# First block of a gated block kernel: idle transposes at the start, key spreads split over two queues, clears moved behind exponentials

## The reference: what is computed

```python
x = x + tanh(g_xattn) * attention(layernorm(x), ctx_1024, ctx_1024)
x = x + tanh(g_ffn)   * expert_layer(layernorm(x))
# attention: 16 heads of 16 features; queries from layernorm(x), keys and values from ctx
scores = q @ k.T                       # blocks of 128 queries
valid  = causal within the block       # (with the block before, where there is one)
o      = softmax(scores) @ v ; out = o @ wo.T + bo
# expert layer: softmax over 8 experts, the best 2 of them, at most 640 tokens an expert
y = (silu(xn @ Wg.T) * (xn @ Wu.T)) @ W3.T   # D=256, FF=1024
```

## Time and profile before

| | us |
|---|---|
| median of 3 runs | 522.09 |
| lowest and highest | 521.87, 523.62 |
| the profiled execution | 520.82 |
| its span, first to last instruction | 519.1 |
| outside the span (520.82 - 519.1) | 1.7 |

### The profile page before, as it was taken

One profiled execution on the slowest core, in us unless ns is written; L12 is line 12 of the kernel. 1 busy time (PEld: TensorE's weight loads), 2 busy tenths in 40 slices (PEclk: granted clock), 3 DMA queues, 4 the chain that ended last, 5 costly groups with the idle time before them and its releaser, 6 DMA issues.

```text
span 519.1 us, 10685 instructions
## 1 busy us (share of the span) xinstructions
PE 480.4 (93%) x3584; PEld 444.2 (86%) x3584; DVE 352.2 (68%) x864; ACT 295.7 (57%) x747; POOL 189.6 (37%) x257
## 2 busy tenths in 40 slices
PE   5989999999999997399999999999999999999991
PEld 3777888888878776399999999999999999999991
DVE  5597779888897998658775754676744858534340
ACT  5877877687778773437574633555643737324140
POOL 7518455776868477600403031112122030320302
PEclk9999999999999996589999999999999999999996
DMA  5989321414143611272857470465622473200111
GB/s 164 249 189 296 73 42 53 77 61 101 47 79 69 199 62 44 71 265 82 248 161 195 135 193 2 97 222 98 220 38 36 128 188 129 32 11 11 19 12 20
DMA packets 41650, 57.34 MB, mean 110 GB/s; under 512 B 3721, under 2 KB 38576, under 8 KB 39552
## 3 DMA queue, kind: packets, MB, share of 16 engines
q1 hardware_dynamic: 35008, 48.49, 32.0%
q0 software_dynamic: 6144, 8.07, 9.2%
q10 hardware_dynamic: 448, 0.14, 0.2%
HBM read 36.24 MB, written 16.72 MB: 102 GB/s over the span
## 4 chain that ended last, share of the span: by engine, by line
PE 55%; DVE 3%; issue 1%; POOL 1%; DMA 0%; DVEq 0%; ACT 0%; POOLq 0%
PE bank L1489 18%; PE bank L1490 17%; PE bank L1491 17%; PE bank L1483 2%; PE bank L1413 1%; DMA expert_rows<-xr,slotu 0%; POOL out_tokens L549 0%; DVE ysc L1181 0%; DVE xr L841 0%; DVE xr L839 0%; DVE topi L882 0%; DVE pT L945 0%; DVE bXl L1138 0%; DVE top L854 0%; DVE xr L900 0%
## 5 line engine op out<-in xcount | busy, mean ns | idle before, releaser
L549 POOL DMA_INDIRECT out_tokens<-ysc,rows x32 | 50.1, 1567 | 242.3 <-DVE ysc L1181 235.8
L1490 PE MATMUL bank<-bXl,wh 128*128 128x384 f32 (+1 forms) x384 | 121.8, 317 | 0.6 <-issue 0.6
L1489 PE MATMUL bank<-bXh,wh 128*128 128x384 f32 (+1 forms) x384 | 121.9, 318 | 0.3 <-DVE bXl L1138 0.3
L1491 PE MATMUL bank<-bXh,wl 128*128 128x384 f32 (+1 forms) x384 | 121.8, 317 | 0.0
L762 ACT ACTIVATE sil<-bank 128x384 f32<-128x384 f32 (+1 forms) x96 | 43.8, 456 | 125.9 <-PE bank L1491 125.8
L1160 DVE TENSOR_TENSOR hF<-sil,bank 128x384 f32<-128x384 f32 (+1 forms) x96 | 48.9, 510 | 75.5 <-ACT sil L762 75.2
L633 ACT ACTIVATE p<-bank,nm 128x128 f32<-128x128 f32 x256 | 73.6, 383 | 26.3 <-DVE nm L940 26.2
L1489 PE MATMUL bank<-wh,hH 128*128 128x256 f32 x256 | 73.8, 288 | 0.3 <-DVE ysc L1181 0.3
L1491 PEld LDWEIGHTS bank<-bXh,wl 128*128 128x128 f32 x384 | 72.6, 189 | 0.7 <-issue 0.7
L1489 PEld LDWEIGHTS bank<-bXh,wh 128*128 128x128 f32 x384 | 72.7, 189 | 0.5 <-issue 0.5
L1490 PEld LDWEIGHTS bank<-bXl,wh 128*128 128x128 f32 x384 | 72.7, 189 | 0.0
(11 more groups left out here) (144 smaller groups left out, 829.6 us busy)
## 6 DMA issues: line engine op xcount, KB each, us to landing
stage<-in_w12T SPq DMA_DIRECT2D x16, 1024.0 KB, 4.9
stage<-in_w3T SPq DMA_DIRECT2D x8, 1024.0 KB, 5.6
expert_rows<-padrow SPq DMA_DIRECT2D x8, 662.5 KB, 8.6
rows<-expert_rows SPq DMA_DIRECT2D x7, 662.5 KB, 4.3
kM<-k SPq DMA_DIRECT2D x62, 64.0 KB, 2.4
cT<-in_ctxT SPq DMA_DIRECT2D x8, 256.0 KB, 3.3
out_tokens<-x_all SPq DMA_DIRECT2D x8, 256.0 KB, 2.3
x_all<-in_x SPq DMA_DIRECT2D x2, 640.0 KB, 5.3
```

The costliest lines, as they stand in the source:

```text
L549: pool.indirect_dma_start(out=out, out_offset=bass.IndirectOffsetOnAxis(rows[par][:, c, D + E:ROW].bitcast(U32), 0), in_=ysc[par][:, c, :] ...
L1489: nc.tensor.matmul(out_ap, ah, bh, start=start, stop=False)
L1490: nc.tensor.matmul(out_ap, ah, bl, start=False, stop=False)
L1491: return nc.tensor.matmul(out_ap, al, bh, start=False, stop=stop)
```

## The change

Four things in the first block, none in the later ones:

1. TensorE gets idle transposes (`keep_running`) into bank Tb[0]: 6 behind the wait for the identity and ahead of the first keys, 1 between keys and input columns, and 4 between input columns and queries.
2. Spreads 6 and 7 of block 0 are issued by ScalarE and no longer by SyncE; each of the two issues 4.
3. ScalarE's clear of quarter 1 of kM[1]'s low part moves behind the queries.
4. Quarters 2 and 3 are cleared behind the exponentials of groups 0 and 1 in `body(0)`.

```diff
@@ SyncE
             sp.wait_ge(km_zero[0], 3)
-            spread_keys(0, 0, (0, 1, 4, 5, 6, 7))
+            spread_keys(0, 0, (0, 1, 4, 5))
             load_w(wo, woT, ld_wo)
@@ ScalarE, body
                     if cur:
                         exps(G, g, not prev1 and g < 2)
+                    if g < 2 and cur and not prev1:
+                        zero_low_keys(2 + g)
                     if g == 0 and cur:
                         values2(n, par)
@@ ScalarE, ahead of body(0)
             act.wait_ge(dve_kl, 1)
             act.wait_ge(km_zero[0], 3)
-            for a in (2, 3):
+            for a in (2, 3, 6, 7):
                 r = slice(a * HD, (a + 1) * HD)
-                act.dma_start(kM[0][r, :, a:H:HR, :].bitcast(F32), k2[r, :, :, :].bitcast(F32)).then_inc(ld_km[0], 16)
-            zero_low_keys(1)
+                act.dma_start(kM[0][r, :, a:H:HR, :].bitcast(F32), k2[r, :, :, :].bitcast(F32)).then_inc(ld_km[a // GH], 16)
             act.wait_ge(bias_ok, 1)
             queries(0, 0, Q0)
-            zero_low_keys(2)
+            zero_low_keys(1)
             values(0, Xo)
             values1(0, 0)
-            zero_low_keys(3)
             body(0, 0, False, False, True, True)
@@ TensorE
             pe.wait_ge(ident_ok, 1)
+            keep_running(Tb[0], 6)
             pe.wait_ge(ld_wk, 16)
             keys(0, 0, K0, 1)
+            keep_running(Tb[0], 1)
             input_columns(0, True, False)
+            keep_running(Tb[0], 4)
             pe.wait_ge(ld_wq, 16)
             queries(0, Q0)
```

## The result

| | before | after |
|---|---|---|
| median of the runs, us | 522.04 (4 runs) | 525.35 (4 runs) |
| lowest and highest | 521.87, 523.62 | 525.06, 525.82 |
| the profiled execution | 520.82 | 525.06 |
| its span | 519.1 | 523.4 |

The ratio of after to before is 1.0057, 95% interval 1.0036 to 1.0078. The change makes the kernel 2 to 3 us slower. Forecast was 521.8 with a range of 520.7 to 523.2; the measured median lies above it.

A forecast was written before the change was run, and what follows sets the result against it. TensorE was taken as bound once dense, some 25 to 27 us in. A 1.0 us lead at exponentials 0, mostly paid back by two clears, left 0.25 us: 522.09 - 0.25 = 521.8 us, range 520.7 to 523.2.

The forecast's parts named there:

- the dense point: Where TensorE's list becomes dense, some 25 to 27 us in; only moving it was to count, 0.25 us earlier.
- The idle transposes' own cost: First block, TensorE: waits for weights, x and queries hide the eleven transposes, cost taken as 0.
- the gain by the clock: Block 0's queries on TensorE: clock rises before them, so 1.97 us instead of 3.75; upper bound 1.8 us taken.
- The rest of the chain: First block, ScalarE and TensorE: spreads issued by 14.17, exponentials 0 at 18.06, pT at 24.6, block 1's queries at 27.0.
- Landing of the spreads: Block 0's spreads 0 to 3 land by 15.9 us, before scores at 16.1; up to 0.4 us allowed.
- payback step: ScalarE behind exponentials 0: two clears of 0.97 us each use up 1.13 us of slack; pT only 0.25 us earlier.
- The issue of spreads one after another: Rival, first block: shared generator issues eight spreads in turn, pT 2.4 us later, 524.5 us; chance 0.04.
- SyncE's pace: First block: SyncE's six spreads issue at 0.74 us each throughout, so both engines issue at the same time.
- The clock late: Rival, first block: clock does not rise before the queries while clears remain, 0.6 us later, 522.7 us; chance 0.22.
- The lead carried: Rival: the 1.0 us lead at exponentials 0 goes through to the end, 521.1 us; chance 0.15.
- Something not seen: Rival: an effect outside the listed cases, no size given; chance 0.04.
- The forecast's list of what would prove it wrong: Block 1's queries moved over 0.8 us, or such a difference only at the attention-expert pause, 195 to 225 us.

The follow-up runs named there:

- after_again: The changed kernel, unaltered, compared a second time with the kernel before: 523.32 against 521.13 us, ratio 1.0036.
- only_placed: Kernel before with 22 wait-only instructions ahead of TensorE's first work: 523.55 against 521.15 us, ratio 1.0046.
- no_idle: Changed kernel without its eleven idle transposes, compared with the kernel before: 521.33 against 521.15 us, ratio 1.0014.
- only_idle: Kernel before with the eleven idle transposes and nothing else of the change: 521.53 against 521.15 us, ratio 1.0005.
- idle_clears: Kernel before plus idle transposes and moved clears, spreads unmoved, wide idle products at 219 us bringing expert code back: 521.14 against 521.97 us, ratio 0.9977.
- after_code_back: Changed kernel with most old idle transposes at 219 us replaced by three wide products, against the kernel before: 520.35 against 521.13 us, ratio 0.9980.
- idle_spreads: Kernel before plus the eleven idle transposes and spreads 6 and 7 on ScalarE, clears unmoved: 524.54 against 521.13 us, ratio 1.0068.
- placed_10_late: Kernel before with 10 wait-only instructions in TensorE's idle wait at 215 to 219 us: 522.62 against 521.97 us, ratio 1.0003.
- code_back_only: Kernel before with most idle transposes at 219 us replaced by three wide products, expert code 40 instructions earlier: 525.29 against 521.97 us, ratio 1.0044.
- placed_22_late: Kernel before with 22 wait-only instructions in TensorE's idle wait at 215 to 219 us: 523.55 against 521.97 us, ratio 1.0017.
- placed_90_further: Changed kernel with 45 more tiny products (90 instructions) ahead of body(0), compared with the kernel before: 525.37 against 521.15 us, ratio 1.0083.

## Why the prediction was wrong

**The step that failed first** is the sentence that the change is worth what it moves the dense point "and nothing else in the 520 us". The idle transposes' own cost was put at 0, with the wait for the weights as their cover. As work that is right: the keys start at 5.54. As code they push every later jump 22 instructions on. Taken between the starts of the two matmuls at the border, less the 0.17 us of one, the hole costs 2.43 and 2.66 us in after and after_again, and 0.75, 0.32 and 0.41 in the three profiles of before: means of 2.55 and 0.49. Missing term: +2.1 us.

**The step that failed second** is the gain by the clock. I read from one execution that the first block runs at the low clock up to 14.8 us, and took that for the kernel. In eight profiles of kernels whose first block has the order of before and no transposes, the queries of block 0 took 1.97 us (once 1.96) in six and 3.5 to 3.75 us in two. Queries of block 1 started at 25.9 to 26.2 in five of the six (26.74 in only_placed, which has its extra waits) and at 27.25 and 27.75 in the two. The mean of the eight is 26.5. With transposes the queries were at 1.97 in all eight profiles, so they may well make the clock sure, but eight of eight against six of nine does not prove it. And the 1.8 us that I counted for it are there only in the executions in which the clock would have come late, here 2 of 8 (3 of 9 with no_idle).

**The rest of the chain held.** Four spreads on ScalarE end at 14.17 (forecast), queries at 14.28 (measured). Scores 16.1, and 16.30. Exponentials 18.06, and 18.24. pT of group 1 24.6, and 24.82. Queries of block 1 27.0, and 27.20, 27.21, 27.32, 27.00 in the four kernels that have the whole first block of the change. Only the mark that they are measured against was wrong: not 27.25, but 26.5 on average. So the dense point moves by +0.7 us and not by -0.25. Even against its own mark of 27.25 the gain was 0.05 us in the profile of after. Landing of the spreads was put at 15.9 with up to 0.4 allowed on top, and all of that was needed: the scores wait for the last one to 16.3. From issue to landing (min/median/max) SyncE's spreads took 3.6/3.9/4.0 us in after, against the 2.4/2.7/3.7 of the earlier trace rows. Taken one by one, the two that SyncE issued beside ScalarE's in the kernel before took 3.6 and 3.7 us, the third 3.0, and the last three, issued alone, 2.4 to 2.5. With four on each queue all of them have company. This cost only 0.1 us, since the queries' low part allows the scores at 16.2 in any case.

**Part by part**, from only_idle's 26.03: the clears' move gives 26.67 (idle_clears), the split added to it 27.20. Both parts cost. The clears cost 0.76 us because two of them (1.94 us) go into 1.1 us of slack, as the prediction's payback step worked out. The split costs 0.5 us because ScalarE comes to its queries later (14.28 against 12.93): their low part ends at 16.10 in after, where idle_clears has it at 14.76 and waits for the spreads up to 15.77. In after_again and after_code_back, too, it is this low part that the scores wait for (16.31 and 16.10), and the late landing adds 0.1 us in after. Beside unmoved clears it costs 2.2 us (idle_spreads), of which 0.3 are a late start and 0.8 the fallen clock.

**The sum as it should have been:** +0.7 and +2.1 make +2.8 us, where 3.3 and 2.2 were measured in the two comparisons. The sum is an estimate: its marks are means over single profiled executions.

**The rivals.** The issue of spreads one after another falls: four spreads took 2.88 us on ScalarE, 0.72 each, while SyncE issued its own at 0.77 each, against 0.70 and 0.74 in the earlier trace rows; the exclusive generator of which the Trainium skill tells in Perfetto Trace Analysis (DMA Instruction, HWDGE) does not show at this pace. One reading of the prediction was too coarse, though: SyncE's pace was not the same over all six. The first three took 0.75 to 0.85 us each and the last three 0.60 to 0.63. Whether ScalarE's issues beside them made the first ones slower, these runs do not tell: in after the fourth took 0.60 us while ScalarE was still issuing. The clock late did not come true in any profile of the change. The lead carried did not either. "Something not seen", given 0.04, was the case. The forecast's list of what would prove it wrong named 195 to 225 us as the place; the hole is 30 us behind that. And the row that was to show the forecast wrong, the queries of block 1, stood at 27.20 in after, 0.2 us from its forecast: it was no guard against a loss that comes later.

**What belongs to one execution.** In the first profile of after, TensorE waits at 216.76 where before had 214.72:

```profile
216.76 0.59 PE L1471 MATMUL bank<-member,onesb 128*128 128x8 bf16 x16 [2.29 <-DVE slotu L935]
```

In after_again, the same kernel:

```profile
214.62 0.59 PE L1471 MATMUL bank<-member,onesb 128*128 128x8 bf16 x16 [0.88 <-DVE slotu L935]
```

Behind the long one VectorE starts 1.4 us late on a finished product. It stands in four of 17 profiles (after, placed_10_late, code_back_only, idle_clears), half of it in a fifth (placed_22_late), and the other twelve have 0.88 or 0.89. The kernels with and without it don't fall apart by the change. What makes it stays open. So does what sets the clock's rise at 223 to 227 us, which moves the first expert matmuls by up to 0.6 us.

**What the terms leave.** Worked out in the same way, from the row of block 1's queries, the hole and the fallen clock where there is one, the medians of all compared kernels but the first after lie lower than the terms give, by 0.2 us (idle_spreads) to 1.0 (only_placed) and 1.2 (only_idle). One cause may be the mark: the three profiled executions of before took 520.82, 519.65 and 521.20 us, on average 0.8 us under the medians that belong to them (522.04, and 520.97 twice), so that the rows describe a kernel before that is faster than its median. The waits of 1.4 us above may be another, as they also fall on kernels whose code up to there is that of before (placed_10_late, code_back_only). Neither was measured.

## What to carry to other kernels

Instructions that cost no engine time still move all code behind them, and here the 22 of the idle transposes cost 2.1 us in the expert layer, some 240 us behind the edit. Where a kernel has jumps, look ahead of such a change at every jump for a hole named "issue" and at how much work stands between it and the hole, and compare kernels whose later code stands at the same place (here three wide products in place of many small ones bring the code back). Before a gain is taken from the clock at the start, profile the kernel before more than once: a low clock that two of eight executions show is worth a quarter of what one row says. And a clear or an issue moved into slack costs what it exceeds the slack by, even if it was hidden where it stood.

## What the runs showed of the hardware

- Behind a taken jump TensorE needed 2.6 to 3.0 us before it got past the next block border, in eleven of eleven profiles; the hole is what the work in between leaves of it.
- A jump whose target block had not been asked for cost 2.94 us at once (code_back_only), and 2.86 us in placed_90_further; in both the packet of instructions starts behind the last matmul ahead of the jump.
- A hole of this size can take the clock with it. Behind holes of 2.27 (only_placed), 2.86 (placed_90_further) and 2.94 us (code_back_only) the granted clock was 0.50 for some 3 us, which cost 1.4 to 1.7 us more, counted between the starts of the matmuls; behind holes of 2.27 and 2.49 us in after and after_again, and of 2.16 to 2.39 in idle_spreads, placed_22_late and only_idle, the matmuls kept their 0.34 us. The size of the hole alone does not decide it (2.27 us with and without).
- The clock of the first 15 us differs between executions of one kernel: queries of block 0 took 3.75, 1.97 and 3.54 us in three profiles of before. The windows print 1.00 there in either case.
- Spreads that SyncE issued beside ScalarE's landed after 3.6 to 4.0 us (before and after), and those that it issued alone after 2.4 to 2.5 us (before).
